# First attention with eight heads in flight and a lag of three slots, a norm behind the copies in VectorE's queue, and a hint on the backward jump of every loop

## The reference, cut to what matters

```python
x = layernorm(x + attention(x))        # 32 query heads of 16, 8 key/value heads, causal, rotary
x = layernorm(x + sparse_ffn(x))       # per block of 32 of 1,792 columns only the argmax column counts
x = layernorm(x + state_space(x))      # Mamba2-like: 128 heads of 64, 8 groups, chunks of 128, gated, RMS norm
x = layernorm(x + ternary_ffn(x))      # 1,376 inner columns, silu(gate) * up
```

```python
scores = q @ k.T / 4; scores = where(causal, scores, -inf)
attn = softmax(scores)                 # exponentials, row sums, division
out = attn @ v                         # then all heads @ Wo
```

## Time and profile before

| | |
|---|---|
| three runs | 2509.47, 2508.31, 2499.82 us; median 2508.31 |
| the profiled execution | 2507.97 us, of which the span is 2506.2 us |
| mean granted clock of PE | 0.951 |
| busy: PE, DVE, ACT, POOL | 2290.8, 1690.9, 1384.0, 844.8 us |
| instruction fetches | queue 8: 108 packets, 1.77 MB; queue 14: 117 packets, 0.96 MB |

### The profile page before, as it was taken

How to read it: one execution, slowest core, us unless ns; L and a number is a source line. 1 busy time by engine, 2 the same in 40 slices (tenths; PEclk the granted TensorE clock), 3 DMA queues, 4 the chain that set the end, 5 groups by cost and what they waited for, 6 DMA issues and landing times. The chain is left out here.

```text
span 2506.2 us, 38276 instructions
## 1 busy us (share of the span) xinstructions
PE 2290.8 (91%) x11624; PEld 1637.8 (65%) x11624; DVE 1690.9 (67%) x2933; ACT 1384.0 (55%) x3121; POOL 844.8 (34%) x681
## 2 busy tenths in 40 slices
PE   6898988897999899899989999999998999987998
PEld 4554544445677676777767767676776767756877
DVE  3465555555796598489579759848966985975345
ACT  4553534314784586378368548738845864862330
POOL 4352423211353154144325414423432542441130
PEclk8699998998999899999999999999999999998999
DMA  5000000001110110111101011011101101102100
GB/s 224 10 1 9 1 1 1 1 0 61 62 31 18 52 35 27 44 30 31 42 30 35 19 48 34 28 44 30 31 15 57 30 28 47 30 1 85 42 17 34
DMA packets 38241, 85.55 MB, mean 34 GB/s; under 512 B 3584, under 2 KB 5888, under 8 KB 37376
## 3 DMA queue, kind: packets, MB, share of 16 engines
q1 hardware_dynamic: 38016, 82.82, 10.0%
HBM read 79.92 MB, written 2.88 MB: 33 GB/s over the span
## 5 line engine op out<-in xcount | busy, mean ns | idle before, releaser
L1623 PE MATMUL b_ps<-xh_keep,wh 128*128 128x512 f32 x1152 | 495.8, 430 | 22.4 <-issue 20.3
L1625 PE MATMUL b_ps<-xh_keep,wl 128*128 128x512 f32 x1152 | 468.8, 407 | 0.0
L1624 PE MATMUL b_ps<-xl_keep,wh 128*128 128x512 f32 x1152 | 468.1, 406 | 0.0
L1414 DVE TENSOR_TENSOR decayed<-decay,b_scores 128x768 f32<-128x768 f32 x256 | 397.9, 1554 | 26.0 <-ACT decay L1142 25.1
L1303 POOL TENSOR_TENSOR wl<-wraw,wh 128x512 fp32r<-128x512 f32 x144 | 190.5, 1323 | 606.6 <-ACT wh L1091 606.6
L1378 DVE SCALAR_TENSOR_TENSOR xs<-b_ps,par,xs 128x510 f32<-128x510 f32 (+2 forms) x384 | 284.9, 742 | 119.4 <-ACT xs L1110 106.4
L1136 ACT ACTIVATE decay<-b_ps,cs 128x256 f32<-128x256 f32 (+1 forms) x1024 | 345.0, 424 | 8.1 <-PE b_ps L1633 7.9
L1623 PEld LDWEIGHTS b_ps<-xh_keep,wh 128*128 128x128 f32 x1152 | 225.2, 195 | 102.1 <-issue 58.3
L1625 PEld LDWEIGHTS b_ps<-xh_keep,wl 128*128 128x128 f32 x1152 | 224.6, 195 | 54.3
L1624 PEld LDWEIGHTS b_ps<-xl_keep,wh 128*128 128x128 f32 x1152 | 226.0, 196 | 43.2
L1504 DVE SCALAR_TENSOR_TENSOR yl<-yg,par,yh 128x512 fp32r<-128x512 f32 x128 | 96.4, 758 | 202.5 <-ACT yh L1157 201.4
(11 more groups left out here) (223 smaller groups left out, 4100.9 us busy)
## 6 DMA issues: line engine op xcount, KB each, us to landing
wraw<-win_dram SPq DMA_DIRECT2D x144, 256.0 KB, 2.6
oraw<-wout_dram SPq DMA_DIRECT2D x8, 2048.0 KB, 8.9
w<-w_dram SPq DMA_DIRECT2D x2, 3584.0 KB, 23.4
fraw<-wgu_dram SPq DMA_DIRECT2D x11, 512.0 KB, 3.5
draw<-wd_dram SPq DMA_DIRECT2D x1, 2816.0 KB, 12.1
xT<-xT_dram SPq DMA_DIRECT2D x4, 512.0 KB, 3.7
x_keep<-x_dram SPq DMA_DIRECT2D x1, 2048.0 KB, 11.5
out_dram<-x_keep SPq DMA_DIRECT2D x8, 256.0 KB, 2.0
```

Source lines behind the costliest of these rows:

```text
L1414: nc.vector.tensor_tensor(sd[:, b % 2, :, :], ex[:, b % 2, :, :], sm[:, b, :].unsqueeze(1).to_broadcast([P, 2, 3 * P]), ALU.mult)\
L1623: nc.tensor.matmul(out, w_h, x_h, start=(k == 0), stop=False)
L1624: nc.tensor.matmul(out, w_h, x_l, start=False, stop=False)
L1625: last = nc.tensor.matmul(out, w_l, x_h, start=False, stop=(k == KT - 1))
```

## The change

Three things change. (1) In stage -1 alone, `ring` is eight heads: two more places for `su`, and two for the probabilities in `hm`; `lag` is three slots, so the transposes of pair d - 3 come in slot d, and the products with the values in odd slots from 5 on; the stage has 20 slots; and DVE makes both copies to `pT`, while ACT makes none.

```diff
-        su = sb("su", [P, PR, 2])
+        su = sb("su", [P, PR + 2, 2])
+        def ring(a):
+            return PR if a else PR + 2
+        def lag(a):
+            return 2 if a else 3
+        def prob(a, n):
+            r = n % ring(a)
+            return (pr[:, r, :] if r < PR else hm[:, (r - PR) * 3 * P:(r - PR + 1) * 3 * P]), su[:, r, :]
+        def slots(a):
+            return PAIRS_OF + (3 if a is None else lag(a) + 1)
@@ PE, each slot
-                        if d >= 4 and d % 2 == 0:
-                            weigh(att, (d - 4) // 2)
-                        if 2 <= d < PAIRS_OF + 2:
-                            turn_probabilities(att, d - 2)
+                        back_d = d - lag(att)
+                        if back_d >= 2 and back_d % 2 == 0:
+                            weigh(att, (back_d - 2) // 2)
+                        if 0 <= back_d < PAIRS_OF:
+                            turn_probabilities(att, back_d)
@@ ACT
-                if n >= PR:
-                    act.wait_ge(*bk.filled((a, "pT", n - PR)))
+                if n >= ring(a):
+                    act.wait_ge(*bk.filled((a, "pT", n - ring(a))))
...
-                        if 2 <= d < PAIRS_OF + 2:
-                            n = 2 * (d - 2)
+                        back_d = d - lag(att)
+                        if att and 0 <= back_d < PAIRS_OF:
+                            n = 2 * back_d
@@ DVE, each slot
                         invert(att, d)
+                    if att is not None and 0 <= d - lag(att) < PAIRS_OF:
+                        if not att:
+                            keep_turned(att, 2 * (d - lag(att)))
+                        keep_turned(att, 2 * (d - lag(att)) + 1)
+                    if nxt is not None and 1 <= d <= 4:
+                        rotate(nxt, *QKV[d - 1])
                     if ffn is not None and d == 12:
                         fed(b, 0)
-                    if att is not None and 2 <= d < PAIRS_OF + 2:
-                        keep_turned(att, 2 * (d - 2) + 1)
-                    if nxt is not None and 1 <= d <= 4:
-                        rotate(nxt, *QKV[d - 1])
@@ all ten loops, PE's of the state-space layer here
-            with pe.Fori(0, LOOPS) as i:
+            with nc.Fori(0, LOOPS, engines=bass.OrderedEngineSet([pe.engine]), hint_back_edge=True) as i:
```

More of the change, by code:

```diff
@@ L368, in turn_probabilities @@
                     pe.wait_ge(*divided1.made((a, n)))
-                    transposes((a, "pT", n), f"t{n % 2}", [pr[:, n % PR, c * P:(c + 1) * P] for c in range(3)])
+                    transposes((a, "pT", n), f"t{n % 2}", [prob(a, n)[0][:, c * P:(c + 1) * P] for c in range(3)])
             def weigh(a, T):
@@ L444, in _ @@
             for b, att, ffn, nxt in stages():
-                for d in range(SLOTS):
+                for d in range(slots(att)):
                     q, i = d // 4, d % 4
@@ L606, in exponentials @@
             def exponentials(a, n):
[L607 to L609 removed]
+                j = n % 4
+                p_, s_ = prob(a, n)
+                if n >= ring(a):
+                    act.wait_ge(*bk.filled((a, "pT", n - ring(a))))
                 act.wait_ge(*bk.drained((a, "s", n)))
[L611 to L614, removed]
+                nc.scalar.activation(p_[:, 0:P], sm[:, j, 0:P], ACT.Exp, bias=mn[:, j, 0:1], scale=-1.0, accum_out=s_[:, 0:1])
+                nc.scalar.activation(p_[:, P:3 * P], sm[:, j, P:3 * P], ACT.Exp, bias=mn[:, j, 1:2], scale=-1.0,
+                                     accum_out=s_[:, 1:2]).then_inc(exp_done.sem, 1)
             act.wait_ge(prepared, 3)
@@ L634, in _ @@
                             for n in (2 * d, 2 * d + 1):
-                                nc.scalar.activation(pr[:, n % PR, 0:P], pr[:, n % PR, 0:P], ACT.Copy, scale=su[:, n % PR, 0:1])\
+                                p_, s_ = prob(att, n)
+                                nc.scalar.activation(p_[:, 0:P], p_[:, 0:P], ACT.Copy, scale=s_[:, 0:1])\
                                     .then_inc(divided0.sem, 1)
@@ L641, in _ @@
                         evacuate((b, "hT", d // 4, 1), hT[:, 4:FT0, :], cols=(FT0 - 4) * P)
-                    if att is not None and d >= 6 and d % 4 == 2:
-                        u = (d - 6) // 4
+                    if att is not None and back_d >= 4 and back_d % 4 == 0:
+                        u = (back_d - 4) // 4
                         act.wait_ge(*bk.filled((att, "av", u)))
@@ L701, in invert @@
             def invert(a, d):
-                r = 2 * d % PR
+                r = 2 * d % ring(a)
                 dve.wait_ge(*exp_done.made((a, 2 * d + 1)))
@@ L1063, in _ @@
             load_in(0, AHEAD - 1)
-            with sp.Fori(0, LOOPS) as i:
+            with nc.Fori(0, LOOPS, engines=bass.OrderedEngineSet([sp.engine]), hint_back_edge=True) as i:
                 ph = Phase("loop", i, i)
@@ L1281, in _ @@
             unit0(ph, 0)
-            with act.Fori(0, LOOPS) as i:
+            with nc.Fori(0, LOOPS, engines=bass.OrderedEngineSet([act.engine]), hint_back_edge=True) as i:
                 ph = Phase("loop", i, i)
@@ L1344, in _ @@
                 weights_lo(0, n)
-            with pool.Fori(0, LOOPS) as i:
+            with nc.Fori(0, LOOPS, engines=bass.OrderedEngineSet([pool.engine]), hint_back_edge=True) as i:
                 ph = Phase("loop", i, i)
@@ L1597, in _ @@
             times_dt(ph, 0, 0, 1)
-            with dve.Fori(0, LOOPS) as i:
+            with nc.Fori(0, LOOPS, engines=bass.OrderedEngineSet([dve.engine]), hint_back_edge=True) as i:
                 ph = Phase("loop", i, i)
@@ L1900, in _ @@
             sp.dma_start(draw[:], io["wd"]).then_inc(loaded, 16)
-            with sp.Fori(0, PAIRS - 1) as i:
+            with nc.Fori(0, PAIRS - 1, engines=bass.OrderedEngineSet([sp.engine]), hint_back_edge=True) as i:
                 load(i, 2)
@@ L1943, in _ @@
             act.wait_ge(scales, 1)
-            with act.Fori(0, PAIRS) as i:
+            with nc.Fori(0, PAIRS, engines=bass.OrderedEngineSet([act.engine]), hint_back_edge=True) as i:
                 ph = Phase("loop", i, i)
@@ L1972, in _ @@
             split(0, 0)
-            with pool.Fori(0, PAIRS) as i:
+            with nc.Fori(0, PAIRS, engines=bass.OrderedEngineSet([pool.engine]), hint_back_edge=True) as i:
                 split(i, 1)
@@ L2016, in _ @@
             nc.vector.tensor_tensor(sc[:, 2, :], sc[:, 0, :], sc[:, 1, :], ALU.mult).then_inc(scales, 1)
-            with dve.Fori(0, PAIRS) as i:
+            with nc.Fori(0, PAIRS, engines=bass.OrderedEngineSet([dve.engine]), hint_back_edge=True) as i:
                 ph = Phase("loop", i, i)
@@ L2062, in _ @@
                 pe.wait_ge(*bk.drained(ph, f"xT{t}"))
-            with pe.Fori(0, PAIRS) as i:
+            with nc.Fori(0, PAIRS, engines=bass.OrderedEngineSet([pe.engine]), hint_back_edge=True) as i:
                 ph = Phase("loop", i, i)
```

5 lines of the change are left out of this document (2 added, 3 removed).

## The result

The changed kernel takes 2484.82 us (median, 2483.36 to 2485.67), the kernel before 2507.34 in the same comparison. The ratio is 0.9925, with a 95% interval from 0.9907 to 0.9943: 14 to 23 us faster. Forecast was 2461, a gain of 47 us. The time lies inside the stated range, but the gain is less than half of what was forecast.

The account below looks back on a forecast made before the run. PE was taken as the bound, through stretches where it stands still or runs at half clock. 2508.0 - 47 (jumps) + 1.7 (first attention) - 2 (norm) = 2460.7, predicted 2461 us; range 2450 to 2488, chance 0.82.

Parts of the forecast that it names:

- Part 1, the gap: State-space loop: hints on the backward jumps remove PE's six "issue" waits ahead of the first matmul, 20.3 us.
- Part 1, what lies beyond the gap: State-space loop: the hint also removes PE's half-speed stretch after each jump, 4.5 us, for six 27 us.
- 7.9 a jump: State-space loop: full cost of an unhinted jump, idle time and half-speed stretch together, 28.1 - 20.2 us, all taken as saved.
- gap gone, clock not: State-space loop: idle time goes, but the clock dip has another cause, such as waits for ACT; 2487 us, chance 0.07.
- Part 1, the short loop and the exit: Ternary feed-forward's loop gains 0; hint instructions cost 0, 1 us either way; untaken target at exits 0, +8 for the range.
- the penalty rival: Loop exits: the hint names a target that isn't taken, costing like a jump without its code, 7.9 us; chance 0.08.
- The rival built on it: Loop jumps: hints are inert, nothing fetches a loop's head early and the six gaps stay; chance 0.14.
- The rival "slower": Whole kernel: the change makes it slower; chance 0.04.
- Part 2: First attention, 31 to 106 us: longer cycles +1.8, earlier start -2.2, longer end +2.1, sum +1.7 us (-2.8 to +3.9).
- Part 3: Slot 12 of three stages: norm behind head 21's copy on DVE; 16.1 us wait becomes 3.6 gained, clock leaves -2 us.

Follow-up runs that it names:

- Parts 2 and 3 together: The changed kernel with every hint taken out, leaving first attention and norm, against the kernel before: 2510.93 us, ratio 1.0021.

## Why the prediction was wrong, point by point

**Part 1, the gap: right.** 20.3 us of "issue" became 2.2 in the profile. The 18.1 us gained are a little under the 20.3 taken, since a hinted jump still leaves 0.3 to 0.4 us.

**Part 1, what lies beyond the gap: the failed step.** It is the term 7.9 a jump, of which 4.5 x 6 = 27 us were aftermath, taken whole on the ground that "After the exit the trace shows the answer for the same instructions". The six jumps took 29.3, 28.1, 28.3, 28.1, 28.4 and 28.1, that is 170 us, before and 136 after (sum of the six spans above), 34 us saved against 47. Of these 18 are the gap and 16 the aftermath, against 27. The aftermath was taken for one thing with one cause, and it is two. From the pass's first matmul to the end of the first wait for ACT the six jumps took 58.0 us before and 47.8 after: that is the stretch right behind the gap, which the hint took whole, 10 us. From there to the last transposes they went from 85.3 to 79.5: 6 us, where the forecast needed the other 17. The exit was a bad yardstick for two reasons that the later runs showed. First, the second slow stretch follows PE's own waits for ACT, which stand in a pass with or without a stall before it; filling them took it away with the stall still there. Second, the exit was one case and no sample. In the profiles of the kernels whose jumps have their gap and whose halves are in their old place, each pass from the second jump on repeats the one before to some tenths of a microsecond, and the exit is clean every time (20.2 us). With hints the passes have another length, and a jump takes 20.9 to 23.8 us; the exit takes 23.1 and 23.0 in the changed kernel and with ten hints alone, and stays at 20.2 to 20.3 with five hints and with one. That the exit itself had PE wait for ACT as often, at a granted clock of 1.00, was read as proof that these waits are harmless. It was luck of the moment at which they fell; what about the moment decides it no run shows. The rival "gap gone, clock not" at 2487 had the cause of the second stretch and 0.07 of the chance, but it left the first stretch standing too. That the measured 2484.8 lies beside it is partly luck: the hints alone saved 26 us against its 20, and attention and norm gave 5 back. The time also lies in the stated range, and that shows nothing for the mechanism either: the range reached up to this rival. Its lower end, 2450, isn't the sum of what it names, which is 2460.7 - 4.5 - 3 - 8.5 = 2445.

**Part 1, the short loop and the exit: partly wrong.** The jumps of the short loop gained nothing, as taken. But the price of a hint, put at 0 with 1 us either way, showed at that loop's entry: 4.0 us of "issue" instead of 2.7, and a slow stretch behind it in the changed kernel (first matmuls of 0.56 to 0.63 us), 2.5 us together in the two profiles. The exit cost 2.9 us more in the profile (20.2 to 23.1), not as a stall, which the penalty rival expected, but through the clock. That rival is out as well, since the kernels with five hints and with one leave the loop in 20.2 to 20.3 us.

**The rule on fetching.** The Trainium skill (Runtime: NRT & Kernel Launch, Instruction fetch mechanics) states that prefetch is purely sequential. For a jump with a hint the trace does not agree: the six gaps fall from 3.4 to 0.4 us, so the head of the loop was there when PE jumped. The rival built on it, 2508 us, is out. The rival "slower" is out as well: no "issue" wait appeared inside a pass.

**Part 2: right in the cycle and near in the sum, not in its terms.** The cycle grew from 7.8 to 8.26 us against 8.25 forecast: products start at 76.89 and 85.15.

```profile
76.89 1.08 PE L401 MATMUL a_ps<-pT,vx 128*32 128x256 f32 x8 [1.57 <-DVE pT L727]
...
85.15 1.08 PE L401 MATMUL a_ps<-pT,vx 128*32 128x256 f32 x8 [1.07 <-DVE pT L727]
```

The start gained more than the 2.2 us forecast and the end cost more than the 2.1: PE's scores of slot 15 start 3.8 us earlier in the changed kernel (91.12 against 94.91), and from them to the last products it is 12.9 us against 9.7. The last products, which were to come about 2 us later, start at 104.06 against 104.63. Two more profiles with the old attention, those of the ten hints and of the norm, have them at 102.6 and 101.6, so a single profile can't settle the sum. The three edits of this stage together cost 2 us (0 to 4.5), forecast +1.7. The lag alone gave nothing that can be measured, against up to 2.5 us forecast in its expectation. The copies alone were worse than worked out.

**Part 3: right in its mechanism, slightly too high.** The wait of 5.39 us turned into two as described, at the places described. The 1.2 us gained a stage were there at the products (1.4 in stage 0), and the clock took them all back where the prediction let it take a third to a half: 0 (-3 to +3) for the norm alone, forecast -2 (-5 to +3). Parts 2 and 3 together cost 5 us (3 to 8), 5.6 more than forecast and more than the 2.3 of their single runs; that difference is inside the intervals.

**The sum.** Forecast: -20.3 - 27 + 1.7 - 2 = -47. Shown by the two profiles, of 2506.2 and 2483.3 us of span: gap -18, aftermath -16, exit +2.9, short loop's entry +2.5, all the rest +5.7, which is the attention's +2.1 up to the loop and slow stretches in and behind it: -22.9.

## What to carry to other kernels

When a stall and a low mean clock stand together, cut the window small enough to see how many slow stretches there are, and where each begins: here one began right behind the stall and went with it, and one began behind two later waits of 1.6 and 1.4 us and stayed. A clean stretch elsewhere in a strictly periodic trace is one observation, however often the period repeats it. Announce the backward jump on the engine that is the bound and whose gap shows as "issue", and fill that engine's waits behind it with work that is ready: here one line and two moved calls gave 41 us, where ten hints, a reworked attention and a moved norm gave 19.

## What the runs showed of the hardware

- A backward jump of PE in the long loop leaves 3.1 to 3.7 us of nothing, and 0.3 to 0.4 us when it is announced. In the short loop it leaves no gap either way.
- A gap of 3.1 to 3.7 us was followed by a slow stretch right away at all six jumps of the kernel before and at five of six with the halves moved; it cost 1.55 us at the second jump. With a hint it appeared at none.
- Two waits of PE, mostly of 1.6 and 1.4 us, were followed by a slow stretch at all six jumps of the kernel before, at five of six of the changed kernel, and not at the exit of the kernel before.
- A hint costs something where the short loop is entered behind a wait: its first matmul comes 0.9 us later, counted from the transposes ahead of it.
- Moving two halves of a pass gained 20 us without and 15 us with PE's hint (0.9896 against 0.9837), so the two gains add up within their intervals or a little short of it.
- The slow stretches make a kernel's time move by itself: the state-space loop's first matmul stood at 628 us in the profile of the kernel before and at 624 to 627 in five of the six hinted kernels whose attention is the same, at 620 in the sixth. The granted clock ahead of it moves along: 0.90 over the first 617 us of the kernel before, 0.91 in the sixth. A change of a few microseconds in this kernel is to be read from medians of many runs, not from one trace.
